# Half of the odd blocks' one-hots on ScalarE, five tiles' similarities in the attention stage, and a changed beginning

## The reference

```
x = x + xattn(layernorm(x), ctx, ctx)              # 16 heads of 16, softmax over 512 keys
y = layernorm(x)                                   # input of the expert layer
xn = y * rsqrt(mean(y*y) + eps) * norm_w
q = xn @ wq;  sim = q . keys                       # 8 heads x 2 halves x 64 keys
s1, s2 = top 16 of each half;  best 16 of the 256 sums -> expert numbers, scores
h = gelu(xn . expert_down[number]) * relu(score)   # 8 x 16 experts of 4096 per token
x = x + sum(h * expert_up[number])
```

## Time and profile before

| | |
|---|---|
| median of three runs | 1099.14 us (1098.94 to 1099.47) |
| the profiled execution | 1095.13 us, of which the span is 1093.3 us |
| TensorE, VectorE, ScalarE, GpSimd busy | 92%, 81%, 36%, 57% of the span |
| attention stage | 0 to about 396 us |
| blocks without hidden or output (`kk == -1`) | about 396 to 446 us |
| loop with hidden, coefficients and output | about 446 to 1043 us, then hidden and output alone |

### The profile page before, as it was taken

The page is one execution under the profiler, slowest core; times in us unless marked ns, Lnnn a source line. Parts: engine busy times, 40 slices in busy tenths (PEclk is TensorE's granted clock), DMA queues, the critical chain, the costliest instruction groups (busy, mean ns, idle before and its releaser), DMA issues.

```text
span 1093.3 us, 27473 instructions
## 1 busy us (share of the span) xinstructions
PE 1004.2 (92%) x10080; PEld 719.1 (66%) x10080; DVE 884.2 (81%) x4242; ACT 393.5 (36%) x739; POOL 628.2 (57%) x790
## 2 busy tenths in 40 slices
PE   6799999988778775799999999999999999999998
PEld 3434444333223245688888788888888888888887
DVE  2677576999999987999989999999999899944211
ACT  2266666555554642222322222222222222222211
POOL 4340340442123127789768888887887788877411
PEclk9699999989998987799999999999999999999999
DMA  4754324233121035200001000000100100110000
GB/s 148 197 145 137 104 89 155 66 119 94 55 75 51 30 114 205 92 7 24 22 18 29 16 24 28 12 28 13 32 23 2 38 28 2 33 33 2 1 20 10
DMA packets 59798, 63.52 MB, mean 58 GB/s; under 512 B 7152, under 2 KB 56048, under 8 KB 59152
## 3 DMA queue, kind: packets, MB, share of 16 engines
q1 hardware_dynamic: 57744, 60.19, 17.6%
q10 hardware_dynamic: 1920, 1.57, 0.7%
HBM read 42.21 MB, written 19.53 MB: 56 GB/s over the span
## 4 chain that ended last, share of the span: by engine, by line
PE 76%; DVE 16%; issue 3%; ACT 2%; DMA 1%; SPq 1%; ACTq 0%; POOL 0%; DVEq 0%; POOLq 0%
PE bank L1425 72%; DVE mem L1330 5%; PE bank L1428 4%; DVE mem L1379 1%; DVE mem L1176 1%; DVE mem L1175 1%; DMA parts_d<-mem 1%; DVE mem L1237 1%; ACT mem L981 1%; DVE mem L1172 1%; DVE mem L1180 1%; DVE mem L1184 0%; SPq L500 0%; DMA mem<-in_ctx 0%; ACTq L995 0%
## 5 line engine op out<-in xcount | busy, mean ns | idle before, releaser
L1425 PE MATMUL bank<-mem 128*128 128x32 bf16 (+6 forms) x9600 | 956.9, 270 | 46.5 <-DVE mem L1330 13.0
L1425 PEld LDWEIGHTS bank<-mem 128*128 128x128 bf16 (+4 forms) x9600 | 667.7, 122 | 290.6 <-issue 107.7
L854 POOL TENSOR_TENSOR mem<-mem 128x1536 bf16<-128x1536 bf16 x121 | 333.5, 2761 | 74.6 <-PE bank L1425 39.4
L1330 DVE TENSOR_REDUCE mem<-bank 128x1 f32<-128x512 f32 x256 | 165.9, 682 | 60.7 <-PE bank L1425 60.1
L981 ACT ACTIVATE mem<-bank 128x512 f32<-128x512 f32 x256 | 147.5, 603 | 136.6 <-PE bank L1425 135.4
L1379 DVE TENSOR_TENSOR mem<-mem,bank 128x2048 bf16<-128x2048 bf16 x128 | 155.0, 1212 | 48.7 <-PE bank L1425 47.9
L1042 ACT COPY mem<-bank 128x512 f32<-128x512 f32 x128 | 74.9, 585 | 103.6 <-PE bank L1425 103.6
L1428 PE MATMUL bank<-mem 128*128 128x128 f32 (+3 forms) x480 | 73.9, 283 | 39.3 <-DVE mem L1108 12.3
L861 POOL TENSOR_TENSOR mem<-mem 128x512 f32<-128x512 f32 x64 | 81.6, 1274 | 49.5 <-ACT mem L1031 49.5
L1428 PEld LDWEIGHTS bank<-mem 128*128 128x128 f32 (+3 forms) x480 | 54.4, 139 | 80.1 <-issue 41.4
L1031 ACT ACTIVATE mem<-bank 128x512 f32<-128x512 f32 x64 | 38.3, 598 | 157.6 <-PE bank L1425 157.6
(11 more groups left out here) (109 smaller groups left out, 705.2 us busy)
## 6 DMA issues: line engine op xcount, KB each, us to landing
mem<-parts_d SPq DMA_DIRECT2D x168, 64.0 KB, 2.2
parts_d<-mem SPq DMA_DIRECT2D x16, 384.0 KB, 3.3
mem<-in_L_ffn_expert_down SPq DMA_DIRECT2D x16, 256.0 KB, 3.3
downT_d<-mem SPq DMA_DIRECT2D x16, 256.0 KB, 3.3
mem<-downT_d SPq DMA_DIRECT2D x4, 1024.0 KB, 8.4
mem<-in_L_ffn_expert_up SPq DMA_DIRECT2D x4, 1024.0 KB, 12.0
tok_d<-mem SPq DMA_DIRECT2D x16, 160.0 KB, 1.8
mem<-tok_d SPq DMA_DIRECT2D x16, 160.0 KB, 2.3
```

Of the source, the lines that this page charges most:

```text
L854: nc.gpsimd.tensor_tensor(ow[q % 2], i0, i1, ALU.mult).then_inc(ow_rdy, 1)
L1330: nc.vector.tensor_reduce(nmx[g % 2][:, i % TB, i // TB:i // TB + 1], psum[n % 3][:, :], AX.X, ALU.max, negate=True).then_inc(s_max, 1)
L1425: return nc.tensor.matmul(o, l, r, start=first, stop=last)
```

## The change

ScalarE makes half of the large one-hots of every odd block: tokens 8 to 15, in two pieces of four tokens, one in the step before the block's own and one in that step. For each token it takes |number - code| over the 128 numbers (Abs with the negated code as bias) and then, for four tokens at once, relu(1 - that). VectorE makes tokens 0 to 7 only. TensorE waits for both. The similarities of tiles 4 to 8 become events of the attention stage (`EARLY`: slot, then the step of each half). ScalarE copies them to a buffer, SyncE stores them in DRAM (`sim_d`) and loads each tile's into `sim` when the tile before has been searched. TensorE issues 34 matmuls of 128 x 128 bf16 at the very beginning, whose results nothing reads. `max_parts(g)` moves to the end of slot `g`, ahead of the picking tasks of step 15. The key stacks of slot 2 are issued at step 0 of slot 1, not at step 8 of slot 0.

```diff
+        EARLY = ((12, 9, 13), (13, 12, 15), (15, 9, 12), (16, 10, 13), (17, 6, 10))
+        NS = NA + len(EARLY)
...
+            for tile, (slot, *at) in enumerate(EARLY, NA):
+                if g == slot:
+                    ev += [(at[n], "early", (tile, n)) for n in range(2)]
...
-        SIM_AT = (2, 4)
+        CLOCK_UP = 34
...
+        def high_ready(eng, c):
+
+            eng.wait_ge(oh_rdy, c + 1)
+            if c % 2:
+                eng.wait_ge(near_rdy, c + 1)
...
+            def load_early_input(i):
+
+                sp.wait_ge(xn_wr[0], 16 * ((NA + i) // TB + 1))
+                sp.wait_ge(xn_wr[1], 16 * ((NA + i) // TB + 1))
+                if i:
+                    wait_filled(sp, "early", (NA + i - 1, 1))
+                sp.dma_start(xs_early, xn_d[:, :, (NA + i) * P:(NA + i + 1) * P]).then_inc(early_ld, 16)
+
+            def store_early(i):
+
+                for n in range(2):
+                    wait_taken(sp, "early", (NA + i, n))
+                    sp.dma_start(sim_d[i, :, n * 512:(n + 1) * 512], sim_early).then_inc(early_wr, 16)
+
+            def load_early(tile):
+
+                sp.wait_ge(early_wr, 32 * len(EARLY))
+                sp.wait_ge(st1, FH * tile)
+                sp.dma_start(sim, sim_d[tile - NA]).then_inc(sim_ld, 16)
...
-            load_sim_input(NA)
+            load_early(NA)
             load_down(0)
             load_down(1)
...
+                    for tile in now["bring"]:
+                        load_early(tile)
...
+                elif name == "early":
+                    tile, n = index
+                    at_least(act, early_wr, 16 * (2 * (tile - NA) + n))
+                    nc.scalar.copy(sim_early, ps[:, :]).then_inc(done, 1)
...
-                    if i == 8 and g < 2:
-                        load_keys(g + 2)
+                    if i == 0 and g == 1:
+                        load_keys(2)
+                    if i == 8 and g == 1:
+                        load_keys(3)
...
+            def one_hot_piece(k, par, q):
+
+                c, n, part = (k + 1) * 16 + (q | 1), (k + 1) * 8 + q // 2, q % 2
+                codes, to = minus[n % 2], oh[1]
+                if part == 0:
...
+                    at_least(act, c_mm, c - 1)
+                    high = by_block(tokT[r])[1][:, (q | 1) % BPT, 0, TK // 2:TK]
+                    nc.scalar.activation(codes, high, ACT.Copy, scale=-1.0).then_inc(codes_neg, 1)
+                    act.wait_ge(codes_neg, n + 1)
+                for i in range(part * TK // 4, (part + 1) * TK // 4):
+                    t = TK // 2 + i
+                    nc.scalar.activation(to[:, t // PAIR, :, t % PAIR], iota[:, :, 0], ACT.Abs, bias=codes[:, i:i + 1])\
+                      .then_inc(distance, 1)
+                act.wait_ge(distance, n * TK // 2 + (part + 1) * TK // 4)
+                near = to[:, (2 + part) * TP // 4:(3 + part) * TP // 4]
+                nc.scalar.activation(near, near, ACT.Relu, bias=1.0, scale=-1.0).then_inc(near_rdy, 1)
...
                     for tile, n in now["mult"]:
                         take_sim(tile, n)
+                    if on(kk, -1, 6):
+                        one_hot_piece(k, par, q)
...
-                    if i == 0 and 1 <= g <= NG:
-                        max_parts(g - 1)
                     if g < NG:
...
+                        if i == 15:
+                            max_parts(g)
...
-                nc.vector.tensor_tensor(oh[q % 2], high.to_broadcast([P, TP, P, PAIR]),
-                                        numbers[:, 0:P, :].unsqueeze(1).to_broadcast([P, TP, P, PAIR]),
+                n = TP // 2 if q % 2 else TP
+                high = by_block(tt)[1][:, q % BPT, 0, 0:n * PAIR].rearrange("p (a t) -> p a t", a=n).unsqueeze(2)
+                nc.vector.tensor_tensor(oh[q % 2][:, 0:n], high.to_broadcast([P, n, P, PAIR]),
+                                        numbers[:, 0:P, :].unsqueeze(1).to_broadcast([P, n, P, PAIR]),
...
+            def turn_clock_up():
+
+                for _ in range(CLOCK_UP):
+                    mm(psum[0][:, 0:P], identb, identb)
+
             pe.wait_ge(consts, 5)
+            turn_clock_up()
...
-                pe.wait_ge(oh_rdy, c + 1)
+                high_ready(pe, c)
...
-                if q in SIM_AT:
-                    similarities(NA, SIM_AT.index(q))
```

More of the change, by code:

```diff
@@ L162, in build @@
         st6e = mem.take(CH * 6).rearrange("p (t c) -> p t c", t=CH)
+        xs_early = mem.take(KD * P).rearrange("p (k t) -> p k t", k=KD)
+        sim_early = mem.take(512)
         mve = [mem.take(CH * 2).rearrange("p (t c) -> p t c", t=CH) for _ in range(2)]
@@ L172, in build @@
         oh = [mem.take(P * TK // 2, BF16).rearrange("p (a c t) -> p a c t", a=TP, c=P) for _ in range(2)]
+        minus = [mem.take(TK // 2) for _ in range(2)]
         oj = [mem.take(OJB * JL * TK // 2, BF16).rearrange("p (a c t) -> p a c t", a=OJB * TP, c=JL) for _ in range(2)]
@@ L432, in walk @@
                        "fetch": [tile + 1 for s, tile, kind, i in tasks
-                                 if s == x and (kind, i) == ("search", 4) and tile + 1 < TILES],
+                                 if s == x and (kind, i) == ("search", 4) and NS <= tile + 1 < TILES],
+                       "bring": [tile + 1 for s, tile, kind, i in tasks
+                                 if s == x and (kind, i) == ("choose", 0) and tile + 1 < NS],
                        "mult": [(tile + 1, x - s) for s, tile, kind, i in tasks
-                                if x - s in (0, 1) and (kind, i) == ("extract", 0) and tile + 1 < TILES],
+                                if x - s in (0, 1) and (kind, i) == ("extract", 0) and NS <= tile + 1 < TILES],
                        "sums": [(tile, 2 * i // FH) for s, tile, kind, i in tasks
@@ L533, in load_sim_input @@
             def load_sim_input(tile):
-                if not isinstance(tile, int) or tile > 0:
-                    sim_filled(sp, tile - 1)
+                if tile:
+                    sim_filled(sp, LAST if tile == NS else tile - 1)
                 sp.dma_start(xs, xn_d[:, :, bass.ds(tile * P, P)]).then_inc(xs_ld, 16)
+            def load_early_input(i):
[12 more added lines that the diff above has]
+                sp.dma_start(sim, sim_d[tile - NA]).then_inc(sim_ld, 16)
             def store_choice(tile):
@@ L601, in _ @@
                         store_choice(tile - 1)
+                for i, (slot, *_) in enumerate(EARLY):
+                    if g == slot:
+                        store_early(i)
+                for i, (slot, *_) in enumerate(EARLY):
+                    if g == slot - 1:
+                        load_early_input(i)
             def load_choice(tile, r):
@@ L1528, in event @@
                         last = mm(ps[:, :], xs[:, k, :], wqk[:, k, n * 512:(n + 1) * 512], k == 0, k == KD - 1)
+                elif name == "early":
+                    tile, n = index
+                    pe.wait_ge(early_ld, 16 * (tile - NA + 1))
+                    for k in range(KD):
+                        last = mm(ps[:, :], xs_early[:, k, :], wqk[:, k, n * 512:(n + 1) * 512], k == 0, k == KD - 1)
                 elif name == "tok":
@@ L1591, in similarities @@
                 if n == 0:
-                    pe.wait_ge(xs_ld, tile * 16 + 16)
-                    if tile > NA:
-                        pe.wait_ge(key, tile)
-                at_least(pe, sim_ev, tile * 2 + (n - 2 * NA))
+                    pe.wait_ge(xs_ld, 16 * (tile - NS + NA + 1))
+                    pe.wait_ge(key, tile)
+                at_least(pe, sim_ev, 2 * (tile - NS) + n)
                 for k in range(KD):
```

24 lines of the change are left out of this document (17 added, 7 removed).

## The result

The change makes the kernel slower by 0.7%: 1104.15 us (median of 7) against 1098.23 us (7 runs of before), a ratio of 1.0069 with a 95% interval of [1.0052, 1.0087]. The forecast of faster was wrong; the direction was rival B's. The profiled execution took 1106.46 us, its span is 1104.6.

The account below looks back on a forecast made before the run. TensorE was taken to bound the loop, VectorE slots 12 to 15, no single engine the 16 steps before the loop. The terms summed to -5.1 us, from 1099.14 to 1094.0 us; range 1083 to 1106.

Parts of the forecast that it names:

- rival B: Slower than before: ScalarE's queue sets the pace wherever a one-hot piece stands behind a copy; 1106 us, chance 0.22.
- Beginning: Start and slot 0: warmed clock speeds TensorE's first work, -2.7 us; moved key stacks end a copy wait, -4.7 us.
- Early tiles in slots 12, 13 and 15: Attention stage: early similarities cost about 1 us per tile in slots 12 and 15, 1.5 in slot 13; +3.5 us.
- Slots 16 and 17: End of the attention stage: early similarities there cost 6.9 us of TensorE, less two idle gaps; +5.9 us.
- `max_parts`: Start of slot 16: splitting the maxima ahead of the picking tasks removes TensorE's 2.8 us wait; -2.8 us.
- ScalarE's stalls: Loop, odd steps: TensorE waits for pieces behind similarity copies (7 x 0.67) and number copies (7 x 0.78); +10.2 us.
- D: ScalarE: a table load for each switch between Exp or Gelu and Abs would add 330 us; chance 0.01.
- The ring before the loop: 16 steps before the loop: ScalarE's chain of coefficients, copies and pieces takes 6.3 us per block pair against 5.39; +3.0 us.
- The loop's saving: Loop: tiles 5 to 8 leave, 4 x 3.45 us of TensorE's work, -13.8 us; shorter VectorE one-hots, -3.7 us.
- VectorE's lateness: Loop: VectorE's shorter one-hots remove TensorE's 3.7 us of unnamed waits for keys and numbers; -3.7 us, from 0.
- Rival C: Early tiles cost in the attention stage what they save, slots 12 to 15 at +9 us; 1099.5 us, chance 0.17.

Follow-up runs that it names:

- start_only: The kernel before plus only the 34 warming matmuls and the moved key stacks; ratio to before 0.9932.
- three_tiles: The change with ScalarE's piece ahead of the copies, pieces only from block 17 on, early tiles only in slots 12, 13 and 15; 1081.64 us, ratio 0.9854.
- start_and_max: The kernel before plus the changed beginning (warming matmuls, moved key stacks) and the earlier `max_parts`; ratio to before 0.992.
- no_early: The change with ScalarE's piece ahead of the copies, pieces only from block 17 on, and no early tile at all; ratio to before 0.9896.
- no_onehots: The change without ScalarE's one-hots, VectorE making all of them; 1093.52 us, ratio to before 0.9974.
- loop_only: The change without ScalarE's pieces in the 16 blocks before the loop, where VectorE makes whole one-hots; 1096.15 us, ratio to before 1.0004.
- onehots_only: The kernel before plus only ScalarE's halves of the odd one-hots; 1118.99 us, ratio to before 1.0209.
- first_and_loop: The change with ScalarE's piece ahead of the copies and no pieces in the 16 blocks before the loop; 1087.07 us, ratio to before 0.9904.
- piece_first: The change with ScalarE's one-hot piece ahead of each step's number and similarity copies instead of behind them; 1093.16 us, ratio to before 0.9978.
- warm_only: The kernel before plus only the 34 warming matmuls; ratio to before 0.9989.

## Why the prediction was wrong

The sum said -5.1; the two profiled spans differ by +11.3, the medians by +5.9, the ratio says +7.6. Point by point:

- **Beginning**: forecast -2.7 - 4.7 = -7.4, measured -7.4 (start_only). The split was off: the keys alone bring 6.1 where I had 4.7, warming alone 1.2 where I had 2.7. That the sum fits is luck in part.
- **Early tiles in slots 12, 13 and 15**: forecast +3.5, not settled: three_tiles has an attention stage of 398.2 us, start_and_max 394.0 (+4.2), but no_early, with the same stage as start_and_max, 398.9 (-0.7).
- **Slots 16 and 17**: forecast +5.9, measured +6.9 in one pair of profiles and 7 to 8 in that stretch.
- **`max_parts`**: forecast -2.8, about -1.4 by the ratios, with overlapping intervals.
- **ScalarE's stalls**: forecast 14 of 0.7 to 0.8 us, +10.2; measured 12 of 0.9 to 1.0, 10.9 us, and some 10 in the loop when they were taken away. The mechanism and the odd steps were right; that the sum was right is luck in part, since the number was too high and the price too low. Two of the seven turns of numbers gave no stall: there TensorE stands 0.89 us for the number copies anyway, as before. A piece took 1.98 us (525.24 to 527.22), not 1.87: Abs follow each other by 0.30 us, not 0.26. The Trainium skill (ScalarE: Activation LUTs, What ACT_TABLE_LOAD costs) gives 280 + 0.833 x 128 - 93 = 294 ns for that spacing and the estimated 2.0 us a piece; the trace agrees with it, and it was nearer than my rows. The trace has no table load for the switches, so D was out.
- **The ring before the loop**: forecast +3.0, measured +7.3 (63.6 against 56.3); the versions that have or lack only the pieces give 6.1 (no_onehots), 6.6 (loop_only) and 8.3 (onehots_only). Between blocks 5 and 13 the pairs cost (457.26 - 430.06) / 4 = 6.80 us, 1.4 more than 5.39, +5.6 where I had +3.7. From block 0 to block 5 it took 22.5 us against 18.7, +3.8 where I had counted -0.7 for the halves on VectorE. Not all of that is the ring's: loop_only and no_onehots, with no piece there, take 20.5 and 20.4, and so does start_and_max, with 20.4. Against these the pieces cost about 2 us there; where the other 1.8 comes from is not shown. After block 13 2.2 come back. This term failed in size by 4.3 us.
- **The loop's saving**: this is the step that failed most. I took -13.8 for tiles 5 to 8, every matmul that leaves as time, and -3.7 for VectorE's lateness: -17.5. With ScalarE's stalls taken away the loop is 9.9 to 10.9 us shorter than before (first_and_loop, piece_first), so some 7 us never came.
  - The -3.7 came to nothing: relief without early tiles leaves the loop as long as it was (no_early, 632.6 against 632.8). Half of these 3.7 us was never VectorE's. The two waits of 0.9 end when ScalarE's number copies do (in the kernel before L895 runs until 805.38 and the transposes start at 805.49), and they grew to 1.1 each with the piece ahead of those copies. The wait of 1.9 us was VectorE's (its keys, L1222, are ready at 604.46 and TensorE starts at 604.57); no_early no longer has it, but has 1.3 us more of waits in the loop's first steps.
  - The -13.8 came only in part: without relief for VectorE the four tiles bring 3.6 (no_onehots), since the loop's waits grow from 4.8 to 12.0 us. With relief they still grow, to 6.5 in first_and_loop and 7.4 in piece_first, at one place where VectorE waits for GpSimd and then GpSimd for VectorE, and the slower clock behind these waits took 1.7 us in some profiles.
  - The rows had given a warning: VectorE was busy 19.17 of 20 us. An engine, or a chain of engines, that follows so closely becomes the bound when the leading one is given 1.73 us back in a step. I priced both edits as if TensorE stayed the bound.

Loop 7, ring 4, and slots, maxima and stalls with 3 to 4 together are 14 to 15 of the 16.4 us between -5.1 and +11.3. That last number is of two profiled executions; by the ratio the gap is 12.7 us (from -5.1 to +7.6), so the terms are good to a few us. Rival B had the right sign and half of the cause: its piece of 1.98 us was below the 2.1 from which it was to decide; what decided was the saving that did not come. Rival C was wrong in place: nothing shows the early tiles of slots 12 to 15 at the 9 us that it needs; it was the loop that did not give back what it should.

## What to carry to other kernels

Work put in an engine's idle time can still cost, if it stands in the queue behind instructions that wait for another engine's fresh result: here the same pieces cost the loop about 10 us behind two kinds of copies and nothing ahead of them. Before work is taken off the bounding engine, look how full the next one is in those very steps, and which chain of engines is ready only just in time; here, with VectorE at 96%, 3.6 of 13.8 us arrived, and relieving VectorE alone brought nothing. Don't put such filler where the steps are short and form a ring (here the 16 blocks without hidden and output): three tiles early, the piece first, and pieces in the loop only, gave 0.9854 [0.9837, 0.9871] where the whole change gave 1.0069.

## What the runs showed of the hardware

- VectorE's comparison of broadcast operands goes mostly by elements: 2048 elements last 1217 ns and 1024 last 683 ns, so 534 ns lie in the second thousand, and an estimated 150 (683 - 534) are fixed.
- ScalarE alternated Abs, Relu, Copy and Gelu in the loop with a single table load of 1283 ns at its start; four Abs of 128 columns with a value per partition took 1.32 us, a Relu of 512 columns 0.63 us.
- TensorE can be slower behind a short wait: 120 matmuls took 9.60 us behind a wait of 1.68 us, at a granted clock of 0.83, and 7.91 us behind one of 1.69 us, at 1.00, in two kernels with the same loop.
- The same 34 warming matmuls lifted different instructions from one execution to the next. The first eight transposes in float32 took 1.95 us in the changed kernel, as without warming, but 1.09 us in start_only and warm_only, which both then waited 1.5 to 1.6 us for the transfer of `in_L_xattn_bk`. Behind that the four float32 matmuls took 1.96 us in the changed kernel and in start_only. In warm_only they took 3.40 us, nearly as long as before, at a granted clock of 0.66 (8.7 to 10.7 us) and 0.50 (10.7 to 12.5 us). All three kernels have the same beginning up to there; why they differ was not settled. The profile's granted clock does not show every slow start: in the kernel before it reads 1.00 beside matmuls of 0.94 us.
